# Attention beside an expert layer: the choice of a batch's experts stands in three parts at other places of VectorE's unit, and the ranks stand behind the transposes of q and k

## The reference

```python
xn = layernorm(x)
# attention: 16 heads of 64
q, k, v = heads(xn @ wqkv.T)
q, k = rope(rmsnorm(q)), rope(rmsnorm(k))
attn = softmax(causal(q @ k.T / 8)) @ v
# experts: each row goes to the one of 8 whose score is highest
scores = xn @ gate_w.T                 # 8 scores a row
chosen = argmax(scores, axis=-1)       # the lowest index among equals
ffn = xn + (xn @ expert_w[chosen].T)
out = x + attn @ wo.T + ffn
```

## Time and profile before

| | |
|---|---|
| median of 3 runs | 1961.97 us (1961.96 to 1962.06) |
| the profiled execution: its own time, and its span | 1962.05 us, 1960.3 us |
| PE busy | 1919.6 us |
| PEld busy | 1676.3 us |
| DVE busy | 1709.1 us |
| ACT busy | 1609.3 us |
| POOL busy | 1393.5 us |
| mean granted TensorE clock | 0.997 of full speed |

### The profile page before, as it was taken

The page is one execution under the profiler, slowest core; times in us unless marked ns, Lnnn a source line. Parts: engine busy times, 40 slices in busy tenths (PEclk is TensorE's granted clock), DMA queues, the critical chain, the costliest instruction groups (busy, mean ns, idle before and its releaser), DMA issues.

```text
span 1960.3 us, 51315 instructions
## 1 busy us (share of the span) xinstructions
PE 1919.6 (98%) x17288; PEld 1676.3 (86%) x17288; DVE 1709.1 (87%) x3916; ACT 1609.3 (82%) x5099; POOL 1393.5 (71%) x2063
## 2 busy tenths in 40 slices
PE   6999999999999999999999999999999999999996
PEld 5788888888888888888888888888888888888885
DVE  6988888888898888888888888989989888898875
ACT  5988888888888888888888888888888888888875
POOL 8878676587756867668775687767877668765854
PEclk9999999999999999999999999999999999999999
DMA  6110211112311132111321112211222212221245
GB/s 211 60 55 20 72 60 55 60 47 80 97 61 50 47 95 93 50 50 53 101 87 61 58 62 81 83 50 64 74 72 77 65 56 66 71 93 50 81 152 159
DMA packets 85138, 145.99 MB, mean 74 GB/s; under 512 B 9872, under 2 KB 63504, under 8 KB 84752
## 3 DMA queue, kind: packets, MB, share of 16 engines
q1 hardware_dynamic: 78736, 125.93, 19.8%
q0 software_dynamic: 6144, 16.79, 2.7%
HBM read 102.05 MB, written 40.63 MB: 73 GB/s over the span
## 4 chain that ended last, share of the span: by engine, by line
PE 94%; DVE 3%; issue 1%; POOL 1%; ACT 1%; DMA 0%; DVEq 0%; POOLq 0%; ACTq 0%
PE ps_g L844 43%; PE ps_g L966 14%; PE ps_g L977 14%; PE ps_s L925 10%; PE ps_g L906 6%; PE ps_g L925 2%; PE ps_s L920 2%; PE ps_g L871 1%; PE ps_g L920 1%; DVE neg_max L1159 1%; PE ps_g L853 1%; DVE prob L1171 0%; ACT prob L709 0%; POOL xn L592 0%; DMA xn<-y_dram,slot_i 0%
## 5 line engine op out<-in xcount | busy, mean ns | idle before, releaser
L562 POOL TENSOR_TENSOR qk_rot<-qk_cos,qk_sin 128x128 f32<-128x128 f32 x1024 | 443.1, 464 | 455.6 <-PE ps_g L906 402.5
L844 PE MATMUL ps_g<-w_qkv,xn_t 128*128 128x384 f32 (+1 forms) x3072 | 634.7, 350 | 2.4 <-DVE xn_t L1071 1.5
L844 PEld LDWEIGHTS ps_g<-w_qkv,xn_t 128*128 128x128 f32 x3072 | 522.3, 189 | 26.1 <-issue 22.6
L568 POOL TENSOR_TENSOR rms_inv<-ss,neg_half 128x8 f32<-128x8 f32 x256 | 425.9, 1664 | 0.0
L709 ACT ACTIVATE prob<-ps_s,neg_max 128x512 f32<-128x512 f32 (+2 forms) x768 | 418.6, 570 | 0.1
L717 ACT ACTIVATE prob_t<-ps_g 128x512 f32<-128x512 f32 (+2 forms) x768 | 394.0, 535 | 9.2 <-PE ps_g L966 7.7
L966 PE MATMUL ps_g<-ident,prob 128*128 128x128 f32 x2560 | 365.6, 273 | 6.5 <-DVE prob L1171 3.4
L573 POOL TENSOR_TENSOR qk_rot<-qk_rot,rms_inv 128x256 f32<-128x256 f32 x512 | 317.8, 642 | 20.0
L966 PEld LDWEIGHTS ps_g<-ident,prob 128*128 128x128 f32 x2560 | 299.9, 141 | 21.4 <-DVE prob L1171 5.9
L1159 DVE TENSOR_REDUCE neg_max<-ps_s 128x2 f32<-128x1024 f32 (+2 forms) x384 | 308.3, 859 | 0.0
L977 PE MATMUL ps_g<-prob_t,v 128*64 128x512 f32 (+3 forms) x2048 | 303.9, 439 | 4.2 <-ACT prob_t L717 3.5
(11 more groups left out here) (122 smaller groups left out, 3045.3 us busy)
## 6 DMA issues: line engine op xcount, KB each, us to landing
w_tile<-w_dram SPq DMA_DIRECT2D x120, 512.0 KB, 3.4
x_rows_s<-x_dram SPq DMA_DIRECT2D x120, 128.0 KB, 2.1
y_dram<-y_rows_s SPq DMA_DIRECT2D x120, 128.0 KB, 1.7
xin<-in_x SPq DMA_DIRECT2D x16, 512.0 KB, 4.0
out<-acc SPq DMA_DIRECT2D x15, 512.0 KB, 2.9
w_dram<-w_tile SPq DMA_DIRECT2D x8, 512.0 KB, 3.0
x_dram<-xn SPq DMA_DIRECT2D x2, 1920.0 KB, 17.6
y_back<-in_expert_t SPq DMA_DIRECT2D x8, 256.0 KB, 4.0
```

The source lines that it names most:

```text
L562: r = pool.tensor_tensor(rot[:, :, a, :], cos[:, :, a, :], sin[:, :, 1 - a, :], ALU.add)
L568: pool.tensor_tensor(rms_inv[:, ts[0]:ts[-1] + 1, :], ss[:, ts[0]:ts[-1] + 1, :], neg_half[:, :, :], ALU.pow).then_inc(s_pool_self, 1)
L844: r = pe.matmul(ps, lhs(a, c), rhs(b, c), start=(c == parts[0] and (a, b) == TERMS[0]), stop=(c == parts[-1] and (a, b) == TERMS[-1]))
```

## The change

`choose` becomes three functions. `choose_top` (top, is_top) moves to the place ahead of the four `row_max`. `choose_lowest` (is_top times below, chosen) moves behind the rope products of tile 1, ahead of `take_projection`. `mark_chosen` (onehot, onehot_b) moves behind `take_projection`. `take_rank` goes behind `take_qk`. On TensorE, and in the list `uses`, `ranks` goes from behind `project` to behind `transpose_qk`. The instructions are the same in number and shape.

```diff
@@ uses
-            if ranks_in(u) is not None:
-                found += ["rank"]
             found += [f"ex{i}" for i in now[1:3]]
             if live(u):
                 found += ["pt0.0", "pt1.1"]
             if live(u + 1):
                 found += ["kt", "qt"]
+            if ranks_in(u) is not None:
+                found += ["rank"]
@@ TensorE, unit
-                if ranks_in(u) is not None:
-                    ranks(u)
...
                 if live(u + 1):
                     transpose_qk(u + 1)
+                if ranks_in(u) is not None:
+                    ranks(u)
                 if live(u + 2):
                     qkv(u + 2, 2)
@@ VectorE, unit
                 if live(u + 1):
                     rope_products(u + 1, 3)
+                if chosen_in(u) is not None:
+                    choose_top(chosen_in(u))
                 if live(u):
                     row_max(u, 0)
...
-                    if pair_of(u) == CHOOSE_PAIR:
-                        choose(b)
-                if u == 1:
-                    choose(0)
...
                     rope_products(u + 2, 1)
+                if chosen_in(u) is not None:
+                    choose_lowest(chosen_in(u))
                 if projection(u):
                     take_projection(u)
-                if ranks_in(u) is not None:
-                    take_rank(u)
+                if chosen_in(u) is not None:
+                    mark_chosen(chosen_in(u))
                 if added_in(u):
...
                 if live(u + 1):
                     take_qk(u + 1)
+                if ranks_in(u) is not None:
+                    take_rank(u)
```

More of the change, by code:

```diff
@@ L249, in ranks_in, with chosen_in @@
             return batch_of(u) // GROUP if live(u) and u % (GROUP * PAIRS) == PAIRS - 1 else None
+        def chosen_in(u):
+            if u == 1:
+                return 0
+            return batch_of(u) + 1 if live(u) and pair_of(u) == CHOOSE_PAIR and batch_of(u) + 1 < B else None
         def slots_in(u):
@@ L1072, in take_xt, with choose_top @@
                                       xn_t[:, 0, c, :].bitcast(F32), ALU.subtract).then_inc(s_xt_lo, 1)
-            def choose(b):
+            def choose_top(b):
                 dve.wait_ge(s_gate, NT * (b + 1))
@@ L1078, in choose, with choose_lowest @@
                                       ALU.is_equal))
+            def choose_lowest(b):
                 own(dve.tensor_tensor(is_top[:, :, :], is_top[:, :, :], below[:, :].unsqueeze(1).to_broadcast([P, NT, E]),
@@ L1081, in choose, with mark_chosen @@
                 own(dve.tensor_reduce(chosen[:, :], is_top[:, :, :], AX.X, ALU.min))
+            def mark_chosen(b):
                 at = b % GROUP * NT
```

## The result

The changed kernel takes 1971.53 us (median of 4 runs, 1971.16 to 1971.92) against 1962.01 for the kernel before: 1.0046 times as long, 95% interval 1.0034 to 1.0058, or 9.5 us more. The span of its profiled execution is 1969.4 us, 9.1 more than before. All executions of these and the later kernels ran at a mean granted TensorE clock of 0.995 to 0.997 of full speed, but for one of the kernel with ScalarE's copies in another order, which took 3102 us at 0.557 and is left out of that kernel's ratio.

A forecast was written before the change was run, and what follows sets the result against it. TensorE and VectorE's chain k_t, q_t, cosine, sine were taken as nearly level, so any delay lengthens a unit. Ranks 5.3 + choice with add_experts 3.3 - units 1 and 7 0.8 = 7.8 us on 1961.97: 1969.8, range 1966.3 to 1973.0.

The forecast's parts named there:

- Ranks, 0.66 in each of eight units: Rank units: tile 2 of qkv takes pt1.1's bank and waits for ScalarE's copy; 0.66 us longer each, 5.3 in all.
- the front: Choice gone from ahead of scale_probs(u, 0): projection no longer waits; at most 0.24 back in units like 31, 0.08 like 23.
- Choice with add_experts, 0.55 in each of six: Units 31, 47, 63, 79, 95, 111: more VectorE work ahead of scale_probs(u, 1), plus GpSimd contention; 3.3 us in all.
- The collision: Units with choice and add_experts: the TENSOR_SCALAR pair moves into GpSimd's rotations and lengthens by 0 to 0.50, taken as 0.25.
- Unit 15, 0: Unit with a choice but neither ranks nor add_experts: VectorE is 0.60 less late there, so no change counted.
- Units 1 and 7, 0.8 back: TensorE's wait for scale_probs(u, 0), 0.49 in unit 1, shrinks: 0.4 us back in each; bounds 0 and 1.6 in all.
- top and is_top at nothing: Their 0.44 us ahead of the row maxima costs nothing, because VectorE waits there for TensorE's scores.
- The bounds: Forecast with its bounds reaches 4.3 to 10.6 us more, the upper from 8 x 0.8 + 6 x 0.7 - 0.
- The reading of a plain unit: Plain unit of 14.78 us: VectorE's sine product of qkv tile 2 sets its end, the next mask product 0.15 behind.
- the bank wait alone: Rival: VectorE's extra work in the six add_experts units is swallowed, only tile 2's bank wait costs; 1967.1 us, chance 0.17.
- The one that ends not slower: Rival: the front's gain stays and tile 2's bank wait is covered; 2.8 us less, 1959.2, chance 0.10.
- Full collision: Rival: pair takes its full 1.25, late for pt2.0 too, ranks' wait at upper bound; 11.8 more, 1973.8 us, chance 0.10.

The follow-up runs named there:

- the front alone: Against the kernel before: only choose_top moved ahead of the row maxima, the other choice instructions and the ranks at their old places; 1961.28 us, ratio 0.9994.

## Why the prediction was right

The forecast was 1969.8, the range 1966.3 to 1973.0; measured were 1971.5. The two large terms were right in mechanism and size, so the hit is not luck; the term for units 1 and 7 was wrong and happened to be small, and the 0.37 of unit 119 was in no term. In sums, the eight rank units lost 5.9 where 5.3 less 0.4 for unit 7 was said, the six units 3.0 where 3.3 was said, and unit 1 gave back nothing instead of 0.4. By its steps:

- *Ranks, 0.66 in each of eight units.* Measured 0.72 in six. The mechanism is shown from three sides: alone it gives the loss, another bank removes it, an earlier copy removes it. Tile 2's start was 0.03 off and tile 3's bound of 0.1 was not needed. Without the wait for pt1.1 a rank unit still lasts 15.20 to 15.22, 0.1 more than before. Part of that is qt's wait for `take_projection`, which the prediction put at 0.21: from the transposes of q and k to the ranks it is 0.94 in the changed kernel and 0.87 with the ranks alone moved, so it is about 0.07, and in the changed kernel the wait for pt1.1 covers it. The 0.08 that the front was to give back in rank units did not show with the front alone.
- *Choice with add_experts, 0.55 in each of six.* Measured 0.50. The order in VectorE's chain gave most. The collision stretched the pair by 0.28 where 0.25 was taken, but its removal gave back only 0.16 of the unit.
- *Unit 15, 0.* Measured 0.06, with the pair at 0.75.
- *Units 1 and 7, 0.8 back.* This term was wrong. Unit 1 gave back 0.06: its wait of 0.49 did vanish, but four of the choice's instructions then stood in its chain. This is VectorE in unit 1 of the changed kernel:

```profile
55.54 0.78 DVE L1087 TENSOR_TENSOR is_top<-is_top,below 128x32 f32<-128x32 f32 x1
...
56.80 0.33 DVE L1095 CAST onehot_b<-onehot 128x32 bf16<-128x32 f32 x1
...
57.24 1.02 DVE L1181 TENSOR_SCALAR prob<-prob,sum_inv 128x384 f32<-128x384 f32 x2
```

  Beside an addition of 1.27 and the rotations on GpSimd, is_top times below took 0.78, onehot_b 0.33 and the pair 1.02; in unit 23 of the same kernel they took 0.18, 0.18 and 0.75. With onehot and onehot_b at the unit's end, unit 1 did shorten by 0.5. The prediction counted the gain at the front of this unit and not the loss at its back, which it had counted for units 31, 47, .... Unit 7 grew by 0.50, where 0.66 - 0.4 = 0.26 was said: the ranks alone made it 0.70 longer, so the choice gave back 0.2 there.
- *top and is_top at nothing.* Almost right, and wrong once. The row maxima came at 1.84 on the unit's clock instead of 1.77. Only in unit 119 was it 2.19, and that unit is 0.37 longer than its siblings in each of the eight kernels that have the front at this place in unit 119, and not in the ones without:

```profile
1807.88 0.19 DVE L1083 TENSOR_TENSOR is_top<-scores_g,top 128x32 f32<-128x32 f32 x1
1808.76 0.69 DVE L1169 TENSOR_REDUCE neg_max<-ps_g 128x2 f32<-128x512 f32 x1 [0.68 <-PE ps_g L931]
```

- *The bounds.* For the upper end the prediction put 0.7 in each of the six units, where its own bound was 0.86. With that it would have been 11.6 above before, 1973.5. It makes no difference to the outcome.
- *The reading of a plain unit.* The prediction says that its end is set by VectorE's sine product, since 0.15 lies between them. The experiment with ScalarE's copies showed that TensorE needs 14.77 anyway. The two are level, so whatever is added to VectorE's chain counts in full, as the prediction used it; but what is taken out of that chain brings next to nothing (0.12 in unit 33 brought 0.02). A constant distance alone did not show which of two waits ended last.

The rivals: the bank wait alone is refuted by the 3.0 us in the six units. The one that ends not slower needed pt1.1's copy earlier. With that copy moved the rank units do fall to 15.22, but not below the 15.10 of before. Full collision had 0.9 for each of the six units and 1.25 for the pair; 0.50 and 1.03 were measured.

## What to carry to other kernels

When a step is moved in a kernel whose buffers go round in the order of use, list for every use between the old and the new place which earlier use's buffer it now takes, and when that one is released. Here the moved step itself was nearly free at its new place, and the step behind it waited 0.45 us for a copy that it had never waited for. Small instructions that nobody waits for belong behind the last link of a chain that is level with the bound, not ahead of it. Before a move is credited with a wait that it removes, follow the same unit to its end.

## What was not expected

- In a unit with top and is_top ahead of the row maxima, the first row maximum starts at 1.84 on the clock whether is_top ended at 1.51 or at 1.66, against 1.77 without them, and in unit 119 at 2.19. Something between the two instructions takes 0.07, once 0.43. In unit 119 TensorE's scores end at 1.73 and GpSimd's instructions stand within 0.01 of where they do in unit 103, so neither is late; the runs don't show what it is.
- GpSimd and VectorE hold each other up: the pair of TENSOR_SCALAR took 0.75 when it began 0.37 before the rotations (unit 33 of the kernel before), 0.96 when it began 0.13 before them, and 1.03 inside them. The four rotations took 1.95 in the first and the last of these cases, and 1.71 where they began only behind the pair.
